# Closing the last head early and preparing the last stage during it

## What is computed

```python
xn = layernorm(x)
# branch 1: dense attention, 16 heads of 16 features, all 2048 keys, a spatial bias on 256 tokens
attn = softmax(q @ k.T * scale + spatial_bias);  out = attn @ v
s = out @ W_proj + b_proj + layernorm(xn) * gamma + beta
# branch 2: two layers on xn; local attention, 8 heads of 64, windows of 128 tokens
for l in range(2):
    h = shift_token(x)
    q, k, v = split(h @ wqkv[l]);  q, k = rotary_xpos(l2norm(q) * qs[l], l2norm(k) * ks[l])
    x = x + local_attention(q, k, v) @ wo[l]          # a token sees its own window and the one before
    h = layernorm(shift_token(x)) * g + b
    a, gate = split(h @ w1[l] + b1[l]);  x = x + (a * gelu(gate)) @ w2[l] + b2[l]
return x0 + s * silu(x)
```

## Time and profile before

| | us |
|---|---|
| median of 3 runs | 3477.18 (3474.28 to 3478.78) |
| the profiled execution, its own time | 3483.3 |
| its span in the profile | 3481.2 |
| PE busy | 3146.6 (90%) |
| DVE busy | 2398.9 (69%) |
| ACT busy | 2248.4 (65%) |
| POOL busy | 857.7 (25%) |

### The profile page before, as it was taken

The page is one execution under the profiler, slowest core; times in us unless marked ns, Lnnn a source line. Parts: engine busy times, 40 slices in busy tenths (PEclk is TensorE's granted clock), DMA queues, the critical chain, the costliest instruction groups (busy, mean ns, idle before and its releaser), DMA issues.

```text
span 3481.2 us, 101232 instructions
## 1 busy us (share of the span) xinstructions
PE 3146.6 (90%) x37288; PEld 2033.7 (58%) x37288; DVE 2398.9 (69%) x4643; ACT 2248.4 (65%) x4655; POOL 857.7 (25%) x952
## 2 busy tenths in 40 slices
PE   5689999999999999999699899998999898998988
PEld 3334444444444444444377777777777777777776
DVE  6688888888889888888555555555555555555554
ACT  2368888888888888888455555555555555555554
POOL 3500000000000000000134433444334443344433
PEclk9889999999999999999899999999999999999999
DMA  4531111111111111111200110001100011010100
GB/s 143 173 138 42 42 38 42 45 42 45 42 45 45 37 41 42 42 45 42 71 16 26 38 36 24 27 26 38 33 25 30 26 38 30 26 30 27 38 27 12
DMA packets 154833, 154.39 MB, mean 44 GB/s; under 512 B 15136, under 2 KB 128120, under 8 KB 154488
## 3 DMA queue, kind: packets, MB, share of 16 engines
q1 hardware_dynamic: 154488, 149.50, 13.3%
HBM read 90.73 MB, written 58.72 MB: 43 GB/s over the span
## 4 chain that ended last, share of the span: by engine, by line
PE 54%; issue 16%; DVE 11%; POOL 9%; ACT 8%; SPq 1%; DVEq 0%; DMA 0%; POOLq 0%; ACTq 0%
PE banks L1291 14%; PE banks L1331 13%; PE banks L1348 13%; PE banks L1529 6%; POOL norms L624 6%; PE banks L1397 3%; ACT masked L846 3%; DVE masked L1109 2%; ACT L879 2%; DVE pT L1057 2%; DVE pT L1158 2%; ACT pT L879 2%; PE banks L1455 2%; DVE masked L1062 1%; DVE pair_max L1009 1%
## 5 line engine op out<-in xcount | busy, mean ns | idle before, releaser
L1009 DVE TENSOR_REDUCE pair_max<-banks 128x1 f32<-128x1024 f32 x1039 | 1260.9, 1223 | 164.7 <-PE banks L1291 112.1
L796 ACT ACTIVATE probs<-banks 128x512 f32<-128x512 f32 x2057 | 1106.8, 602 | 199.2 <-PE banks L1331 163.3
L1291 PE MATMUL banks<-k_aug,q_aug 96*32 96x512 bf16 x8312 | 854.3, 389 | 71.1 <-issue 45.8
L1331 PE MATMUL banks<-q_aug,k_aug 98*32 98x512 bf16 x8228 | 846.8, 388 | 0.0
L1348 PE MATMUL banks<-probs,v_cur 128*32 128x256 f32 x8192 | 639.5, 384 | 0.1
L1291 PEld LDWEIGHTS banks<-k_aug,q_aug 96*32 96x32 bf16 x8312 | 241.6, 97 | 435.7 <-DVE pair_max L1009 213.9
L1331 PEld LDWEIGHTS banks<-q_aug,k_aug 98*32 98x32 bf16 x8228 | 251.8, 97 | 190.4 <-issue 13.9
L846 ACT ACTIVATE masked<-masked,npeak 128x256 f32<-128x256 f32 x512 | 253.8, 496 | 160.2 <-DVE npeak L1109 159.5
L1516 PE MATMUL banks<-hnT,w_sb 128*114 128x128 f32 x3072 | 354.6, 276 | 0.9 <-ACT hnT L869 0.9
L1516 PEld LDWEIGHTS banks<-hnT,w_sb 128*114 128x114 f32 x3072 | 341.7, 179 | 22.0 <-ACT hnT L869 22.0
L1348 PEld LDWEIGHTS banks<-probs,v_cur 128*32 128x32 f32 x8192 | 263.2, 111 | 136.6 <-issue 16.0
(11 more groups left out here) (141 smaller groups left out, 4028.8 us busy)
## 6 DMA issues: line engine op xcount, KB each, us to landing
acc_scratch<-acc_sb SPq DMA_DIRECT2D x128, 256.0 KB, 2.4
heads_win<-acc_scratch SPq DMA_DIRECT2D x512, 64.0 KB
q_aug<-q_parts SPq DMA_DIRECT2D x34, 192.0 KB, 2.8
k_aug<-k_parts SPq DMA_DIRECT2D x34, 192.0 KB, 2.7
q_parts<-parts SPq DMA_DIRECT2D x48, 128.0 KB
k_parts<-parts SPq DMA_DIRECT2D x48, 128.0 KB
x_in<-in_x SPq DMA_DIRECT2D x10, 512.0 KB, 4.0
q_aug<-q_parts SPq DMA_DIRECT2D x34, 128.0 KB, 2.4
```

Of the source, the lines that this page charges most:

```text
L796: nc.scalar.activation(probs[:, step % PRING, :], banks[:, (use - first_use) % SRING, :], ACT.Exp, scale=SCALE).then_inc(prob_ready, 1)
L1009: nc.vector.tensor_reduce(pair_max[:, q, half:half + 1], banks[:, 4 + 2 * (t % 2):6 + 2 * (t % 2), :], AX.XY, ALU.max).then_inc(smax_read, 1)
L1291: last = nc.tensor.matmul(banks[m:m + CT, 4 + t % 4, :], q_aug[0:TERM_ROWS, b, q * P + m:q * P + m + CT], k_aug[0:TERM_ROWS, b, kq * BANK: ...
L1331: last = nc.tensor.matmul(banks[m:m + CT, (use - use_of(first_step)) % SRING, :], k_aug[0:AUG, b, kb * P + m:kb * P + m + CT], q_aug[0:AUG ...
```

## The change

The loop over heads runs 15 times, and the last head follows it as straight code with a flag `ends`. In it, max tiles, row maxima, shift rows, scores and exponentials that belong to a next head are left out; the four last parts of the weighted sums and the last `save_sums` remain. SP's loop runs 15 times too; behind it the eight stores of head 15 are issued without the loads of a next head, and after the fourth of them the two input windows and the first rotary tables are loaded. POOL does everything except the clearing of the first halves of `kT` and `vw` before it adds to `phase2_end`, and then clears only these halves. PE adds to `phase2_end` but does not wait for it; it waits for the things it needs. `wo_sb` gets a semaphore of its own.

```diff
         def turns(engine):
-            yield 0, range(FIRST_STEP)
-            with engine.Fori(0, HEADS) as h:
-                yield h, range(FIRST_STEP, FIRST_STEP + STEPS)
+            yield 0, range(FIRST_STEP), False
+            with engine.Fori(0, HEADS - 1) as h:
+                yield h, range(FIRST_STEP, FIRST_STEP + STEPS), False
+            yield HEADS - 1, range(FIRST_STEP, STEPS + SUMS_STEP + 1), True
...
         # SP
+            for group in range(GROUPS):
+                store_sums(HEADS - 1, group)
+                if group == QC - 1:
+                    for b in range(B):
+                        load_window(0, b)
+                    sp.dma_start(tables[:], rotary[0]).then_inc(tables_in, 16)
             for b in range(B):
-                sp.wait_ge(aug_loaded[b], 16 * 6 * (HEADS + 1))
+                sp.wait_ge(aug_loaded[b], 16 * 6 * HEADS)
             sp.wait_ge(acc_stored, 16 * HEADS * GROUPS + 16)
             sp.wait_ge(phase2_end, 4)
-            sp.dma_start(wo_sb[:], wo.rearrange("l (k p) e -> p l k e", p=P)).then_inc(ff_weights, 16)
+            sp.dma_start(wo_sb[:], wo.rearrange("l (k p) e -> p l k e", p=P)).then_inc(wo_in, 16)
...
             for b in range(B):
-                load_window(0, b)
                 load_heads(0, b)
-            sp.dma_start(tables[:], rotary[0]).then_inc(tables_in, 16)
...
         # POOL
             pool.wait_ge(bias_done, HEADS * 6)
-            nc.gpsimd.sem_inc(phase2_end, 1)
-            pool.wait_ge(phase2_end, 4)
-
-            nc.gpsimd.memset(kT[:], 0.0).then_inc(ff_const, 1)
-            nc.gpsimd.memset(vw[:], 0.0).then_inc(ff_const, 1)
             nc.gpsimd.memset(xT[:, 1], 0.0).then_inc(ff_const, 1)
...
+            pool.wait_ge(ff_weights, FF_WEIGHTS)
+            pool.wait_ge(tables_in, 16)
+            for l in range(LAYERS):
+                rotary_table(l)
...
+            nc.gpsimd.sem_inc(phase2_end, 1)
+            pool.wait_ge(phase2_end, 4)
+            nc.gpsimd.memset(kT[:, :, :, :, 0:WINDOW], 0.0).then_inc(k_zeroed, 1)
+            nc.gpsimd.memset(vw[:, :, :, 0], 0.0).then_inc(v_zeroed, 1)
...
         # ACT
                 for step in steps:
                     group, kb, use = step // KB, step % KB, use_of(step)
-                    act.wait_ge(st_ready, h * ST_USES + (use + 2))
+                    if kb == SUMS_STEP and group > 0:
+                        save_sums(h, group - 1)
+                    if ends and step >= STEPS:
+                        continue
+                    act.wait_ge(st_ready, h * ST_USES + (use + 2 - (ends and step > STEPS - KB + MSTEP)))
...
-                    if kb == MSTEP:
+                    if kb == MSTEP and not (ends and group + 1 == GROUPS):
...
-                    if kb == SUMS_STEP and group > 0:
-                        save_sums(h, group - 1)
...
         # DVE
                 for step in steps:
                     tile = step + LEAD
+                    if ends and tile >= STEPS:
+                        continue
...
         # PE
-                    if step > first_step:
+                    if step > first_step and not (ends and step >= STEPS):
                         scores_to_exp(h, first_step, step)
...
-                    max_tile(h * PAIRS, tile)
+                    if not (ends and tile >= STEPS):
+                        max_tile(h * PAIRS, tile)
...
-                    if kb == MSTEP:
+                    if kb == MSTEP and not (ends and group + 1 >= GROUPS):
                         shift_rows(h, first_step, group + 1, use_of(step) + 1)
 
             pe.wait_ge(pv_done, HEADS * PVH + 1)
-            pe.wait_ge(prob_ready, HEADS * STEPS + (FIRST_STEP + 1))
             nc.tensor.sem_inc(phase2_end, 1)
-            pe.wait_ge(phase2_end, 4)
-            pe.wait_ge(ff_const, 12)
+            pe.wait_ge(prob_ready, HEADS * STEPS + 1)
+            pe.wait_ge(acc_saved, HEADS * GROUPS + 1)
+            pe.wait_ge(smax_read, HEADS * PAIRS + 2)
+            pe.wait_ge(ff_const, 10)
             pe.wait_ge(ff_weights, FF_WEIGHTS)
```

More of the change, by code:

```diff
@@ L246, in build @@
         ff_const = sem("ff_const")
+        k_zeroed = sem("k_zeroed")
+        v_zeroed = sem("v_zeroed")
+        wo_in = sem("wo_in")
         tab_ready = sem("tab_ready")
@@ L451, in _, with store_sums, load_window @@
             load_aug(0, 1)
-            with nc.sync.Fori(0, HEADS) as h:
-                next_head = nc.sync.snap((h + 1) % HEADS)
+            def store_sums(h, group):
+                b, qc = group // QC, group % QC
+                sp.wait_ge(acc_saved, h * GROUPS + (group + 2))
+                sp.dma_start(acc_dram[b, bass.ds(h, 1), :, qc * CHUNK:(qc + 1) * CHUNK][0], acc_sb[:]
+                             ).then_inc(acc_stored, 16)
+            def load_window(w, b):
+                sp.dma_start(xT[:, 0, b, :, 1:], xT_dram[:, :, bass.ds(w * WINDOW + b * N, WINDOW)]
+                             .rearrange("k p t -> p k t")).then_inc(x_window[b], 16)
+            with nc.sync.Fori(0, HEADS - 1) as h:
+                next_head = nc.sync.snap(h + 1)
                 for group in range(GROUPS):
-                    b, qc = group // QC, group % QC
                     if group == QC - 1:
@@ L464, in _ @@
                         load_aug(next_head, 1)
[L465 to L467 removed]
+                    store_sums(h, group)
+            for group in range(GROUPS):
[4 more added lines that the diff above has]
+                    sp.dma_start(tables[:], rotary[0]).then_inc(tables_in, 16)
             for b in range(B):
[L469 removed]
+                sp.wait_ge(aug_loaded[b], 16 * 6 * HEADS)
             sp.wait_ge(acc_stored, 16 * HEADS * GROUPS + 16)
             sp.wait_ge(phase2_end, 4)
[L472 removed]
+            sp.dma_start(wo_sb[:], wo.rearrange("l (k p) e -> p l k e", p=P)).then_inc(wo_in, 16)
             for b in range(B):
                 nc.sync.sem_inc(result_stored[b], 16)
[L477 to L480 removed]
             def load_heads(w, b):
@@ L593, in _ @@
             nc.gpsimd.memset(mask[:, WINDOW:], 0.0).then_inc(ff_const, 1)
-            pool.wait_ge(ff_const, 10)
+            pool.wait_ge(ff_const, 8)
             nc.gpsimd.affine_select(out=mask_prev[:], in_=mask_prev[:], compare_op=ALU.is_ge, fill=MASKED, base=0,
@@ L599, in _, with rotary_table @@
                                     base=0, pattern=[[-1, WINDOW]], channel_multiplier=1).then_inc(ff_const, 1)
-            pool.wait_ge(ff_const, 12)
+            pool.wait_ge(ff_const, 10)
+            def rotary_table(l):
+                nc.gpsimd.tensor_tensor(tab[:, l], tables[:], gains[:, l], ALU.mult).then_inc(tab_ready, 1)
+            pool.wait_ge(ff_weights, FF_WEIGHTS)
+            pool.wait_ge(tables_in, 16)
+            for l in range(LAYERS):
+                rotary_table(l)
             for carried in (k_carried, v_carried, x_carried, x1_carried):
@@ L696, in gate_branch @@
                 nc.gpsimd.tensor_tensor(s_win[:, b], s_win[:, b], x_win[:, b], ALU.add).then_inc(result_ready, 1)
-            pool.wait_ge(tables_in, 16)
-            for l in range(LAYERS):
-                rotary_table(l)
             invert_norms(0, 0, 1)
@@ L788, in _ @@
             save_shift(0, 0)
-            for h, steps in turns(nc.scalar):
+            for h, steps, ends in turns(nc.scalar):
                 first_use = use_of(steps[0])
@@ L1029, in _ @@
                 max_pair(0, t)
-            for h, steps in turns(nc.vector):
+            for h, steps, ends in turns(nc.vector):
                 for step in steps:
-                    group, kb = step // KB, step % KB
                     tile = step + LEAD
+                    if ends and tile >= STEPS:
+                        continue
                     if tile % 2 == 1:
@@ L1037, in _ @@
                         split_max(h * GROUPS, tile // KB)
-            dve.wait_ge(smax_read, HEADS * PAIRS + ((FIRST_STEP + LEAD) // 2 + 2))
+            dve.wait_ge(smax_read, HEADS * PAIRS + 2)
             nc.vector.sem_inc(phase2_end, 1)
             dve.wait_ge(phase2_end, 4)
-            dve.wait_ge(ff_const, 12)
+            dve.wait_ge(ff_const, 10)
             dve.wait_ge(ff_weights, FF_WEIGHTS)
@@ L1360, in _ @@
                 max_tile(0, t)
-            for h, steps in turns(nc.tensor):
+            for h, steps, ends in turns(nc.tensor):
                 first_step = steps[0]
@@ L1370, in _ @@
                         pe.wait_ge(aug_loaded[1], h * 96 + 96)
-                    if tile == STEPS:
+                    if tile == STEPS and not ends:
                         pe.wait_ge(aug_loaded[0], h * 96 + 192)
-                    max_tile(h * PAIRS, tile)
+                    if not (ends and tile >= STEPS):
+                        max_tile(h * PAIRS, tile)
                     ago, first, half = PV_PLAN.get(kb, (-2 * GROUPS, 0, 0))
@@ L1433, in scores @@
                 l, b = parts_of(k)
+                if k == 0 and n == 0:
+                    pe.wait_ge(k_zeroed, 1)
```

(4 more changed lines are left out.)

11 lines of the change are left out of this document (4 added, 7 removed).

## The result

The changed kernel takes 3512.41 us (median of 4 runs, 3512.04 to 3515.56), the kernel before 3477.98 (4 runs, 3474.28 to 3479.91). The ratio is 1.0101, with a 95% interval of 1.0087 to 1.0115: **slower by 34.4 us**, where I forecast faster by 34.4. The time is outside the range and on the other side of no change.

What follows compares the result with a forecast made beforehand. It took the seam to be bound by SP's queued issues, the rotary tables landing last before `cross`. Terms 4.6 + 1.5 + 4.8 + 23.4 = 34.3, placed in time 34.4, gave 3477.2 - 34.4 = 3442.8 us, range 3438 to 3451.

Steps and rivals of the forecast that it cites:

- the last group: Head 15's steps 107 to 127 without max tiles: ACT sets the pace, exponentials back to back, gain 1.5 us.
- steps 128 to 136: End of head 15, only four parts of weighted sums and a copy left: 6.9 us becomes 2.0, gain 4.8 us.
- Point (1): Sign at head 15's entry: no 3 us idle piece on PE, 11 us between `save_sums`; wrong if 15.6.
- One turn fewer: Head 15 entered by falling out of the head loop, exit taken as costing 0: gain 4.6 us.
- The seam: Dense attention to last stage, inputs prepared early: 3.3 us to `cross` where 26.7 pass, gain 23.4 us.
- A: Rival: PE's exit from the head loop stalls like a turn, 4.6 us not gained, 3447.4 us; chance 0.11.
- B: Rival: last stage's first item runs at full clock, about 3 us more gained, 3439.8 us; chance 0.09.
- C: Rival: after the seam `wo_sb` or the heads come late, 3448 to 3453 us; chance 0.04.
- D: Rival: longer instruction streams make a moved last-stage loop refetch each turn, slower, 3485 to 3507 us; chance 0.06.
- the five: The rivals: A, B, C, D and one with nothing gained at the seam, given no chance of its own.

Runs made afterwards that it cites:

- the repaired kernel: The changed kernel with the copy of the sums put back behind the exponential of step 6 in all heads: 3446.54 us, ratio to the kernel before 0.9897.

## Why the prediction was wrong

**The term that was missing.** The sum has four terms and none for heads 0 to 14 apart from their turns. Its part on ACT speaks of "the last group" and of steps 128 to 136; the moved `save_sums` was taken for a part of that and never priced for the 15 heads of the loop. It costs 0.6 us in 105 groups of the loop and 0.4 in five straight ones. Counted over the 110 ordinary intervals between copies, the mean is 11.589 instead of 11.005: 64.2 us. At `cross` the trace adds up: 64.2 lost in the groups, 5.6 gained over the 15 turns and entries, 1.3 in the last group, 28.4 from the copy before the last one to `cross`, 0.7 ahead of the first copy; that leaves 28.2 lost, where 28.1 are measured. Point (1) of what would show it asked for "11 us from `save_sums` to `save_sums`" at the entry of head 15; there are 14.24, and 11.40 to 11.60 already in every ordinary group beside it.

The rows of before would have given the price. PE's order in step 6 is scores, max tile, weighted sums; the sums take 0.62 with their end and the exponential of step 6 runs beside them. Putting the copy first makes ACT wait for nearly all of that, 0.5 to 0.6, and 112 groups times 0.5 to 0.6 are 56 to 67 us, well over the gain that I forecast. What had to be asked is what is queued behind the waiting instruction: the exponential of step 6, and behind that PE's next bank. ACT has about 0.95 us of idle pieces in a group, which looks like cover, but they are waits for PE's scores, spread over the group; a delay at one point isn't made good by them. PE itself is busy 10.96 of 11.00 us in a group before, so its 0.43 of waiting is not made good either. The straight head loses about the same as the loop: its groups take 11.40, and 10.88 in the repaired kernel, so 0.52, and ACT's bracket there is 0.52 too. How the 0.6 divides between PE and DVE stays open.

**The terms that I did give**, by the changed kernel's trace:

- *One turn fewer, 4.6.* A turn costs 5.0 on average in the kernel before (15 intervals of mean 16.02 against 11.00); the one turn that I had measured was 15.60. Leaving the loop costs no standstill for instructions, as I took it from the first entry and DVE's exit. But the entry costs 2.8 (14.24 - 11.40), for POOL's bias products and the clock behind them, so the interval fell from 16.02 to 14.24 and the term is 1.8, not 4.6. The prediction wrote "POOL has no bias work after 1638.39 + 2.09" and did not ask what the bias work at the head's start would do. A stall went, and the next late thing took most of its place. In the Trainium skill (Runtime: NRT & Kernel Launch, "Instruction fetch mechanics") fetching runs ahead in sequence, and a taken branch to code outside the part that is held waits for a fetch. The traces agree: 2.98 us of standstill at a turn, none for instructions at the exit, and none in the loop over windows, which fetches nothing.
- *The last group, 1.5.* 9.65 instead of 11.00 between copies: 1.35; 9.42 in the repaired kernel, 1.58. The prediction read the 0.40 of the earlier trace rows as four matmuls at half clock; that row starts at full clock (1597.41 to 1597.61 has PEclk 1.00). Its 0.20 for full speed is still close: a little before the turn four matmuls follow each other by 0.22, behind it by 0.43.
- *Steps 128 to 136, 4.8.* The last exponential ends at 1737.52, POOL is released at 1739.81: 2.3 where 6.9 were: 4.6.
- *The seam, 23.4.* From POOL's release to `cross` 1743.31 - 1739.81 = 3.5 where 26.7 were: 23.2.

Timelines of ACT, POOL and PE of the changed kernel show the last three:

```profile
1731.90 0.58 ACT L793 COPY acc_sb<-banks 128x512 f32<-128x512 f32 x1
1732.38 5.14 ACT L811 ACTIVATE probs<-banks 128x512 f32<-128x512 f32 x10
1739.10 0.58 ACT L793 COPY acc_sb<-banks 128x512 f32<-128x512 f32 x1 [1.59 <-PE banks L1362]
...
1704.84 1.41 POOL L611 TENSOR_TENSOR tab<-tables,gains 128x256 f32<-128x256 f32 x2 [4.14 <-DMA tables<-in_rotary]
1739.81 1.80 POOL L622 MEMSET kT<- 128x2048 f32 x1 [33.56 <-ACTq L820]
...
1740.09 3.67 PE L1413 MATMUL banks<-wqkv_sb,xT 128*128 128x512 f32 x8 [1.06 <-DVEq L1059]
```

The exponentials run back to back, POOL's tables are made 35 us ahead of the seam, the clearing takes 1.8 as half of 3.51, and PE projects at full clock after 1.06 idle. The repaired kernel is 34.8 us below the kernel before on the same chip (3481.3 - 3446.5), where the sum said 34.4. Its trace bears out less: from copy to copy it gains 1.8 at the entry, 1.6 in the last group and 28.8 from the copy before the last one to `cross`, 32.2 in all. So the closeness is partly luck. The other 2.6 are within what turns vary by: the 15 turns of two kernels of equal time, the one before and the one with only POOL's order changed, average 16.02 and 15.72 in their profiles, 4.5 us in all.

**The rivals.** A: PE's exit costs no turn, though the entry costs 2.8 by another way, so its price came true in part without its mechanism. B: PE was idle for 4.10 us and the four transposes took 0.66 instead of 1.11, so the clock had not yet fallen; it fell afterwards, the second item's projection took 4.64 instead of 3.66, and nothing was won. Timeline of PE, the changed kernel:

```profile
1749.58 0.66 PE L1444 MATMUL banks<-ident,pT 128*128 128x128 f32 x4 [4.10 <-DVE pT L1094]
...
1761.77 4.64 PE L1413 MATMUL banks<-wqkv_sb,xT 128*128 128x512 f32 x8
```

C: no wait for `wo_sb`. D: the last stage's loops still fetch nothing, and the stage kept its length within 1.6 us. My chance for slower was right to exist and had the wrong mechanism; the true one was in none of the five.

## What to carry to other kernels

Read a diff of an engine's loop for what it does to every turn, before the turn that it is for: a moved line counts as often as the loop runs, and 0.6 us in each of 110 groups outweighed a seam of 27. A wait moved ahead of an instruction costs what that instruction was covering, so ask what runs beside that wait now. And when a stall is to go, look for work that finishes inside it; that is the next to be late.

## What was unexpected of the hardware

A turn of the loop over heads costs 5.0 us: PE stands still for 3.1 on average (2.98 in the earlier trace rows) and then works at half clock for some 3 us (PEclk 0.50 from 1598 to 1601). An entry in straight code inside the loop body costs 0.4. Holding five heads in the body instead of one took 54 us off a kernel of 3447, or 52 when each is taken against the kernel before on its own chip. At the entry of head 15 the clock was still full when PE restarted at 1653.77 after 1.60 us of idleness, and it fell to half 0.9 us later (PEclk 1.00 to 1654.6, 0.50 from 1654.7). After 1.06 us of idleness at the seam it stayed full, and the projection ran in 3.67.
